# Binary layer of a vision tower: weight products on four 64x64 tiles, 512-wide sign sums, gated signs tripled through DRAM

## The reference, cut

```python
xh = layernorm(h)                                     # 64 channels a token
gate = sigmoid(xh @ proj_w.T + proj_b) > 0.5          # 8 gates a token
w = einsum("be,eio->bio", gate, weight)               # per token a 64 x 64 matrix
y = einsum("bi,bio->bo", sign(xh), sign(w)) * scale
h = h + y
```

## Time and profile before

| | |
|---|---|
| time, 3 runs | 1758.92 us median (1758.51 to 1761.61) |
| span of the profiled execution | 1762.0 us |
| PE, PEld busy | 1600.4, 1209.6 us |
| DVE, ACT, POOL busy | 1205.6, 974.5, 540.3 us |
| mean granted TensorE clock | 0.973 |
| largest line on the chain that ended last | L887, 11% |

### The profile page before, as it was taken

How to read it: one execution, slowest core, us unless ns; L and a number is a source line. 1 busy time by engine, 2 the same in 40 slices (tenths; PEclk the granted TensorE clock), 3 DMA queues, 4 the chain that set the end, 5 groups by cost and what they waited for, 6 DMA issues and landing times.

```text
span 1762.0 us, 87962 instructions
## 1 busy us (share of the span) xinstructions
PE 1600.4 (91%) x32618; PEld 1209.6 (69%) x32618; DVE 1205.6 (68%) x3509; ACT 974.5 (55%) x1893; POOL 540.3 (31%) x699
## 2 busy tenths in 40 slices
PE   6989898779999999999986899999999999999996
PEld 4666666567777777777775666766676666766663
DVE  3878787645565566655554677877778777877762
ACT  2333333234444444444432278888888878888776
POOL 2311111145555555555542212222222212222210
PEclk9999999869999999999998699999999999999999
DMA  5010101034444344443342133333333333333332
GB/s 160 26 30 24 30 24 35 2 102 107 113 114 109 105 111 115 112 115 109 106 117 56 31 81 84 85 85 86 84 83 82 89 83 83 83 85 87 84 77 61
DMA packets 134691, 143.29 MB, mean 81 GB/s; under 512 B 42498, under 2 KB 90114, under 8 KB 134370
## 3 DMA queue, kind: packets, MB, share of 16 engines
q1 hardware_dynamic: 126306, 116.16, 25.3%
q10 hardware_dynamic: 8320, 26.22, 5.2%
HBM read 66.51 MB, written 16.99 MB: 47 GB/s over the span
## 4 chain that ended last, share of the span: by engine, by line
PE 64%; issue 11%; POOL 6%; DVE 5%; SPq 4%; ACT 4%; DMA 4%; POOLq 1%; ACTq 0%; DVEq 0%
PE ps_D L887 11%; PE ps_D L798 4%; PE ps_D L675 3%; PE ps_AV L904 3%; SPq L462 3%; PE ps_J L837 3%; POOL key_patch L561 3%; DMA q_st<-q_d 3%; PE ps_J L995 2%; PE ps_J L963 2%; POOL key_patch L560 2%; DVE tile_a L1285 2%; PE ps_J L945 2%; PE ps_OT L751 2%; PE ps_OT L641 2%
## 5 line engine op out<-in xcount | busy, mean ns | idle before, releaser
L1175 ACT ACTIVATE prob<-ps_D 128x1024 bf16<-128x1024 f32 x448 | 459.5, 1029 | 123.8 <-PE ps_D L887 122.2
L1145 ACT ACTIVATE prob<-ps_D 100x512 f32<-100x512 f32 x256 | 139.0, 595 | 223.2 <-PE ps_D L798 223.2
L1349 DVE TENSOR_REDUCE m_sb<-ps_D 128x4 f32<-128x400 f32 x256 | 135.3, 570 | 126.4 <-PE ps_D L775 126.4
L798 PE MATMUL ps_D<-tile_a,key_patch 64*100 64x128 f32 x2048 | 174.2, 288 | 0.3 <-issue 0.3
L887 PE MATMUL ps_D<-tile_b,w_parts 128*128 128x256 bf16 x1024 | 151.5, 273 | 13.0 <-ACT prob L1175 3.4
L887 PE MATMUL ps_D<-tile_a,w_parts 128*128 128x256 bf16 x1024 | 152.0, 274 | 11.6 <-DVE xg L1471 2.8
L552 POOL TENSOR_TENSOR tile_a<-q_st,q_mask 128x1024 f32<-128x1024 f32 x64 | 123.5, 1930 | 61.8 <-DMA q_st<-q_d 59.5
L798 PEld LDWEIGHTS ps_D<-tile_a,key_patch 64*100 64x100 f32 x2048 | 135.7, 166 | 0.5 <-issue 0.5
L794 PE MATMUL ps_D<-mT,key_rows 64*100 64x128 bf16 x1024 | 120.9, 227 | 7.9 <-issue 7.4
L527 POOL TENSOR_TENSOR rstd_bin<-veps_bin,minus_half 128x2 f32<-128x2 f32 x64 | 44.2, 691 | 267.2 <-DVE veps_bin L1236 267.2
L887 PEld LDWEIGHTS ps_D<-tile_b,w_parts 128*128 128x128 bf16 x1024 | 92.6, 102 | 45.3 <-issue 34.3
(11 more groups left out here) (176 smaller groups left out, 3963.4 us busy)
## 6 DMA issues: line engine op xcount, KB each, us to landing
tile_a<-xg SPq DMA_DIRECT2D x384, 64.0 KB, 2.0
tile_b<-xg SPq DMA_DIRECT2D x384, 64.0 KB, 2.0
key_st<-k_d SPq DMA_DIRECT2D x128, 162.0 KB, 3.0
tile_b<-v_d ACTq DMA_DIRECT2D x128, 120.0 KB
tile_b<-v_d ACTq DMA_DIRECT2D x64, 160.0 KB
w_exp<-experts SPq DMA_DIRECT2D x64, 129.0 KB, 2.3
xT<-in_x SPq DMA_DIRECT2D x32, 256.0 KB, 2.6
k_d<-kpad SPq DMA_DIRECT2D x64, 64.0 KB, 3.0
```

The costliest lines, as they stand in the source:

```text
L798: mm = pe.matmul(s_loc[x][0:NKL, u * P:(u + 1) * P], key_patch[rows_of(x), par, at * NKL:(at + 1) * NKL], q_block[rows_of(x), par, at * P: ...
L1145: act.activation(prob1[0:NKL, 2 * g + x, :], s_loc[x][0:NKL, :], ACT.Exp).then_inc(T2["exp_done"], 1)
L1175: act.activation(sgn[:, k % 4, :], unit(k, par)[:, :], ACT.Sign).then_inc(BN["sign"], 1)
L1349: dve.tensor_reduce(m_sb[:, C * x + HOT[x] + 4 * g:C * x + HOT[x] + 4 * g + 4], m_loc[x][:, 0:4 * NKL].rearrange("p (u n) -> p u n", u=4), ...
```

## The change

- The weight products use four tiles of 64 x 64. Of 64 rows, 48 hold 3 parts of 2 channel lanes x 8 gates; the two row halves hold different channels. A unit is 8 products of 256 columns (2 output halves x 2 lane pairs x 2 row halves) instead of 4. The row half selects the PSUM bank, the lane pair the column half.
- The sign sums take 512 columns: 4 products for two units instead of 8. ysum is 512 wide, its two halves are added by L985's product, now 4 in place of 2.
- xg goes to a DRAM tensor x_d by 2 transfers of 128 KB, and after a wait for both comes back three times by 2 transfers of 384 KB with a repeating source (48 rows of 8 KB each). xg of the next strip waits for the first two only, unit 0 for a semaphore of its own for each buffer.
- The rows to be cleared are now 32 to 63 and 96 to 127 of both tiles: 4 memsets. SP waits for them before its first strip.
- DVE places the weights by 2 multiplies and 4 multiply-adds over 128 rows, with a mask for part and lane.

The diff without the changed declarations of names:

```diff
@@ -108,11 +108,11 @@
     t["keep"] = np.repeat(np.stack([keep, keep * np.float32(ALPHA ** P)])[None], P, 0)
-    group, lane, gate = np.arange(P) // 32, np.arange(P) % 32 // NG, np.arange(P) % NG
-    t["lane_mask"] = (lane[:, None] == np.arange(4)[None, :]).astype(np.float32)
+    half, part, lane = np.arange(P) // 64, np.arange(P) % 64 // 16, np.arange(P) % 16 // NG
+    t["part_mask"] = ((part[:, None, None] == np.arange(3)[None, :, None]) & (lane[:, None, None] == np.arange(2)[None, None, :])).astype(np.float32).reshape(P, 6)
     spread = np.zeros((P, 4, P), np.float32)
     for n in range(4):
-        spread[C + 16 * n + 4 * group + lane, n, np.arange(P)] = 1
+        spread[C + 32 * half + 2 * (4 * part + n) + lane, n, np.arange(P)] = 1
     t["spread"] = spread.reshape(P, 4 * P)
@@ -192,14 +192,14 @@
         x_parts = [tile_a[:, :, :].rearrange("p a n -> p (a n)").bitcast(BF16), tile_b[:, :, :].rearrange("p a n -> p (a n)").bitcast(BF16)]
-        PARTS = 96
-        w_bin, w_rest = key_patch[0:PARTS, :, :].rearrange("p a n -> p (a n)")[:, 0:1024], key_rows[0:PARTS, :, :].rearrange("p a n -> p (a n)")[:, 0:1024]
-        w_high, w_mid, w_sel = rot[0:PARTS, 0, :].bitcast(BF16), rot[0:PARTS, 1, :].bitcast(BF16), q_sb[0:PARTS, :, :].rearrange("p a n -> p (a n)").bitcast(BF16)
-        ysum, ys, yo = sb("ysum", [P, 256], BF16), sb("ys", [P, 2, C]), sb("yo", [P, 2, C])
+        w_bin, w_rest = key_patch[:, :, :].rearrange("p a n -> p (a n)")[:, 0:1024], key_rows[:, :, :].rearrange("p a n -> p (a n)")[:, 0:1024]
+        w_high, w_mid, w_low = rot[:, 0, :].bitcast(BF16), rot[:, 1, :].bitcast(BF16), q_sb[:, :, :].rearrange("p a n -> p (a n)").bitcast(BF16)
+        ysum, ys, yo = sb("ysum", [P, 512], BF16), sb("ys", [P, 2, C]), sb("yo", [P, 2, C])
 
         q_d = nc.dram_tensor("q_d", (NSTRIP, P, P), F32, kind="Internal").ap()
+        x_d = nc.dram_tensor("x_d", (NSTRIP, 2, 16, 4, 1024), BF16, kind="Internal").ap()
         o_v = out.rearrange("b (t p) c -> p (b t) c", p=P)
@@ -456,10 +456,15 @@
                 sp.wait_ge(BN["xg"], times(g + 1))
+                for half in range(2):
+                    sp.dma_start(x_d[bass.ds(g, 1), half, :, :, :].rearrange("a l g n -> g (a l) n"), xg[rows_of(half), :]).then_inc(BN["x_out"], 16)
                 sp.wait_ge(BN["w_ps"], times((g - 1) * 8))
-                for part in range(3):
-                    for n in range(4):
-                        sp.dma_start(x_parts[par][32 * part:32 * (part + 1), 1024 * n:1024 * (n + 1)], xg[32 * n:32 * (n + 1), :]).then_inc(BN["x_in"], 16)
+                sp.wait_ge(BN["x_out"], times((g + 1) * 32))
+                settle(sp)
+                for half in range(2):
+                    src = x_d[bass.ds(g, 1), half, :, :, :].rearrange("a l g n -> (a l) (g n)")
+                    src = bass.AP(src.tensor, src.offset, [[0, 3], [4096, 16], [1, 4096]])
+                    sp.dma_start(x_parts[par][C * half:C * half + 48, :], src).then_inc(BN["x_in%d" % par], 16)
 
@@ -472,6 +477,7 @@
             sp.dma_start(w_bin, a["w_bin"]).then_inc(s_gate_w, 16)
+            sp.wait_ge(s_clear, 4)
             staggered(sp, strips)
@@ -581,10 +587,11 @@
             gp.wait_ge(T2["h_done"], times(NS))
-            gp.memset(tile_a[PARTS:P, :, :], 0.0).then_inc(s_clear, 1)
-            gp.wait_ge(s_clear, 1)
-            gp.memset(tile_b[PARTS:P, :, :], 0.0).then_inc(s_clear, 1)
-            gp.wait_ge(s_clear, 2)
+            for n, (tile, at) in enumerate(((tile_a, 32), (tile_a, 96), (tile_b, 32), (tile_b, 96))):
+                if n:
+                    gp.wait_ge(s_clear, n)
+                gp.memset(tile[at:at + 32, :, :], 0.0).then_inc(s_clear, 1)
+            gp.wait_ge(s_clear, 4)
 
@@ -882,10 +889,12 @@
                     for oh in range(2):
-                        for a in range(2):
-                            at = (2 * (k % 2) + a) * 4 + k // 2
-                            mm = pe.matmul(d[:, a * 512 + oh * 256:a * 512 + (oh + 1) * 256], w_parts[:, at, oh, :, :].rearrange("r i o -> r (i o)"),
-                                           x_parts[half][:, at * 256:(at + 1) * 256], start=True, stop=True)
+                        for lanes in range(2):
+                            for x in range(2):
+                                at = 2 * k + lanes
+                                mm = pe.matmul(d[rows_of(lanes), x * 512 + oh * 256:x * 512 + (oh + 1) * 256],
+                                               w_parts[rows_of(x), at, oh, :, :].rearrange("r i o -> r (i o)"),
+                                               x_parts[half][rows_of(x), at * 256:(at + 1) * 256], start=True, stop=True)
                     mm.then_inc(BN["w_ps"], 1)
@@ -900,9 +909,10 @@
                     for k in (2 * pair, 2 * pair + 1):
-                        for cg in range(4):
-                            mm = pe.matmul(bank["AV"][32 * cg:32 * (cg + 1), 0:256], lane_sum[:, int(k == 1), :], sgn[:, k % 4, cg * 256:(cg + 1) * 256],
-                                           start=k == 0, stop=k == 7)
+                        for oh in range(2):
+                            cg = 2 * (k % 2) + oh
+                            mm = pe.matmul(bank["AV"][32 * cg:32 * (cg + 1), :].rearrange("o (x t) -> o x t", x=2), lane_sum[:, int(k == 1), :],
+                                           sgn[:, k % 4, :].rearrange("r (x h t) -> r h x t", x=2, h=2)[:, oh, :, :], start=k < 2, stop=k >= 6)
                     mm.then_inc(BN["y_part"], 1)
@@ -982,7 +992,9 @@
                     for t in range(2):
-                        mm = pe.matmul(bank["T"][:, 256 + t * C:256 + (t + 1) * C], ysum[:, t * P:(t + 1) * P], half_sum[:, :], start=True, stop=True)
+                        for x in range(2):
+                            mm = pe.matmul(bank["T"][:, 256 + t * C:256 + (t + 1) * C], ysum[:, 256 * x + t * P:256 * x + (t + 1) * P], half_sum[:, :],
+                                           start=x == 0, stop=x == 1)
                     mm.then_inc(BN["y_ps"], 1)
@@ -1040,8 +1052,8 @@
                         pe.wait_ge(s_placed, 13)
-                        pe.wait_ge(s_clear, 2)
-                    pe.wait_ge(BN["x_in"], times((n + 1) * 192))
+                        pe.wait_ge(s_clear, 4)
+                    pe.wait_ge(BN["x_in%d" % (1 - par)], times((n + 1 + par) * 16))
                 if q is not None:
@@ -1179,7 +1191,7 @@
                     act.wait_ge(BN["y_ps"], times(p))
-                    act.activation(ysum[:, :], bank["AV"][:, 0:256], ACT.Copy).then_inc(BN["ysum"], 1)
+                    act.activation(ysum[:, :], bank["AV"][:, :], ACT.Copy).then_inc(BN["ysum"], 1)
                 if f is not None or g is not None:
@@ -1413,17 +1425,18 @@
                     dve.tensor_copy(w_mid, w_rest).then_inc(s_placed, 1)
-                    dve.tensor_copy(w_sel[0:32, :], w_high[0:32, :]).then_inc(s_placed, 1)
-                if j == 2:
-                    dve.wait_ge(s_placed, 7)
-                    dve.tensor_tensor(w_sel[64:96, :], w_rest[64:96, :], w_mid[64:96, :], ALU.subtract).then_inc(s_placed, 1)
-                    dve.tensor_copy(w_sel[32:64, :], w_mid[32:64, :]).then_inc(s_placed, 1)
-                if j == 3:
-                    dve.wait_ge(s_placed, 9)
-                if j in (3, 4):
-                    for lane in (2 * j - 6, 2 * j - 5):
-                        dve.tensor_scalar(w_parts[0:PARTS, :, :, lane, :], w_sel.rearrange("p (n h o) -> p n h o", n=16, h=2),
-                                          lane_mask[0:PARTS, lane:lane + 1], None, ALU.mult).then_inc(s_placed, 1)
+                    dve.wait_ge(s_placed, 6)
+                    dve.tensor_tensor(w_low, w_rest, w_mid, ALU.subtract).then_inc(s_placed, 1)
+                if j in (2, 3, 4):
+                    for lane in range(2):
+                        dve.wait_ge(s_placed, 7 + 2 * (j - 2) + lane)
+                        dst = w_parts[:, :, :, lane, :]
+                        src = (w_high, w_mid, w_low)[j - 2].rearrange("p (n h o) -> p n h o", n=16, h=2)
+                        own = part_mask[:, 2 * (j - 2) + lane:2 * (j - 2) + lane + 1]
+                        if j == 2:
+                            dve.tensor_scalar(dst, src, own, None, ALU.mult).then_inc(s_placed, 1)
+                        else:
+                            dve.scalar_tensor_tensor(out=dst, in0=src, scalar=own, in1=dst, op0=ALU.mult, op1=ALU.add).then_inc(s_placed, 1)
 
@@ -1467,7 +1480,7 @@
                     dve.wait_ge(BN["gates"], times(g + 1))
-                    dve.wait_ge(BN["x_in"], times(g * 192))
+                    dve.wait_ge(BN["x_out"], times(g * 32))
                     dve.tensor_tensor(xg[:, :].rearrange("r (n t) -> r n t", n=4), ring(5, par)[:, :].rearrange("r (n t) -> r n t", n=4),
@@ -1547,7 +1560,7 @@
     arr["b_gate"] = np.tile(n(L1_ffn_proj_b), P // NG).reshape(P, 1)
```

(8 more changed lines are left out.)

## The result

Against 1760.06 us before (4 runs) the changed kernel takes 2405.62 us (median of 4 runs, 2404.75 to 2415.37): a ratio of 1.369, with a 95% interval of 1.366 to 1.372. Forecast was 1746, with a range of 1714 to 1777. The sign was wrong, and the size by a factor that no term of the sum comes near.

The account below looks back on a forecast made before the run. PE, busy 91% of the span, and its in-order queue were taken as the bound. 1762.0 - 15 - 4 + 6.5 = 1749.5 us for the profiled execution, whose span is 3.1 above the median, so about 1746; range 1714 to 1777.

Parts of the forecast that it names:

- Part 3: Tripling xg through DRAM: the trip takes 9.7 us, needed after 13, so hidden; -4 us in all.
- The -4 for both ends: Layer stage's first and last strips: removing the Sync loop saves 2.4 us plus the last unit 0's 1.41 us wait.
- The Sync loop of 11.3 to 12.2: Kernel before: xg, its 12 transfers and their landing take this many us a strip, hidden behind PE except in the last strips.
- Part 1: Weight products as 64x64 tiles: w4 and w7 lose 0.09 us each, w5 and w6 gain 0.11 each, w0, w1, w3 gain.
- Rival 2: Weight products on PE: entering 64x64 tiles costs 0.1 us more in five places, total 1777 us; chance 0.22.
- rival 4: Weight products on PE: only two quadrants run together, 1.2 us more a strip, 1823 us; chance 0.04.
- Part 2: Sign sums 512 wide: sums within 0.02 us of zero, y products +0.06 on PE, ysum +0.21 on ACT.
- The walk: One strip followed step by step: L945 waits for ACT's xs and leads only 0.3 to 0.35 us; period falls 0.24.
- The state step: DVE's step L1487 after xg: L1037 waits for it, leads only 0.2 to 0.3 us and starts 0.11 slower.
- Part 4: Way into the layer stage: two more memsets +3.7 us, DVE's weight placing +2.8, together +6.5.
- -15: Middle of the layer stage: 64 strips, each 0.24 us shorter, save 15 us.
- rival 5: DRAM trip: it takes over 13 us and unit 0 waits in each strip; chance 0.02.

Follow-up runs that it names:

- e5: Changed kernel with the three copies as inner dimension of the return transfers and xg sent out in one 128-row transfer: 1747.47 us, ratio 0.9954.
- e3: Kernel before, 128x128 weight products kept, with xg sent to DRAM in one transfer and back in three, 32 rows outermost: 1745.6 us, ratio 0.9917.
- e7: e6 with the sign sums as before the change, 8 products of 256 columns and ysum 256 wide: 1729.69 us, ratio 0.9854.
- e6: e5 with each tile cleared by one memset over all 128 rows, two instead of four: 1745.8 us.
- e1: Changed kernel with xg sent out in one 128-row transfer and back in six, 16 rows outermost: 1750.01 us, ratio 0.9939.
- e8: e6 with ScalarE's order xfgT, xs, ysum instead of ysum, xfgT, xs: 1741.29 us, ratio 0.9921.
- e10: e7 with ScalarE's order xfgT, xs, ysum, as in e8: 1723.0 us, ratio 0.9819.
- e2: Changed kernel with rows outermost on the way back from DRAM only, the way out left as in the change: 1840.58 us (one run).
- e9: Changed kernel with only the way out to DRAM altered, to one transfer of 128 rows: 2289.0 us, ratio 1.3037.

## Why the prediction was wrong, point by point

**Part 3, the step that failed.** "From the end of xg: 1.4 + 1.1 + 3 + 1.1 + 3.1 = 9.7 us, and w0 needs it 13 us after", hidden "with about 3 us of cover". The 2.7 (3 in the sum) and 3.1 were landings of other transfers, v_d<-v_sb and the load of w_bin, taken over by their bytes alone. The 384 KB of w_bin have 96 rows outermost, those of x_in three copies. In the change the two trips take 11.9 and 17.9 us. The dimension order was in the diff. Two errors lie in that step:
- the landing of x_in: 17.9 for 3.1. Even well shaped it is 5.7 (e5), with 768 KB a strip under way and not the 384 of that row;
- transfers were priced as if each had the engines to itself. x_out, w_exp and the store stand behind x_in in the engines that it fills. "Behind the waiting Sync stand w_exp and the store of y, both due a strip later: hidden" looked at Sync's issue order only, not at what is under way.

With good shapes the step holds: in e5 the trip fits and nobody waits for it. The -4 for both ends was too small. e3, which changes only this, has the same 11.64 us in its middle, but from its first to its last clip (1015.5 to 1739.1) 723.6 us for 732.8. 8.0 of these 9.2 lie in the last seven strips, 71.7 us for 79.7. Whole layer stages, from the first memset on, are 793.2 and 803.0 us: the ends are worth 9.8. The Sync loop of 11.3 to 12.2 held more of the last strips than the xg steps showed.

**Part 1, the units.** Right within 0.02. From start to start, w4: L973 to the unit 0.60 (L963 before: 0.51), the unit 0.34 (0.44), L983 0.54 (0.43), 1.48 for 1.38: it loses 0.10, and 0.09 was forecast. w7 loses 0.10. w5 and w6 gain 0.10 each, for 0.11. From the product ahead of w0 to the sums behind w1 the way is 0.92 for 1.28, a gain of 0.36, for 0.34. A unit is 8 products in 0.34 us, the price of the L904 block (0.33). Rival 2, dearer entries, and rival 4, two quadrants at a time, fall. e7 against e3 is this part alone in the middle of the stage, where neither waits for a transfer: 11.64 to 11.24, 0.40 us a strip.

**Part 2, the sums.** L985 (L996 now) +0.06 as forecast: 0.21 to the next start, 0.15 with two products. ysum 0.59, as taken from L1145. The walk's "new wait, for ACT" is there, 0.35 at L955. Together they take back 0.22 of the 0.40 (e7 to e6). The forecast had 0.24 left, the measurement 0.18.

**The state step** was to gate L1037. It doesn't: in e1 the unit ahead of it (w7) takes 0.34 like the others, and L1049 (L1037 before) starts behind it without a wait for DVE.

**Part 4, the way in.** From the first memset to the first clip pass 58.2 us before, 57.9 in e3, 62.4 in e5 and 63.8 in e1: 4 to 6 us more, for 6.5 forecast. The memsets are 2.6 of it (e6), for 3.7. The rest is taken for DVE's placing, which no run shows apart: e6, with two memsets as in e3, needs 59.9, 1.9 more than e3, for 2.8 forecast; e7, e8 and e10, which place alike, are 0.3 to 2.2 above e3. The first xg was to come 6 us later; from the first memset it is 3.4 later in e5 and 4.8 in e1.

**The sum.** -15, -4 and +6.5 were forecast, -12.5 together; the repaired change measures 7 to 10 less than before (e5, e1). That is close, but by terms that don't agree: e3 alone, the transfers without the tiles, already has 14.8 less (1745.6 against 1760.41), and the tiles with their wide sums add nothing to it. From layer stage to layer stage, e1 against e3: the first 56 periods give 9.7, the way in takes 5.9 more (63.8 for 57.9), the last seven strips 3.2 more (74.9 for 71.7) and what follows the last clip 1.3 more: together 0.6 more by the unrounded times, 793.8 for 793.2 us. The spans, 1749.5 and 1750.7, have it the other way, since the layer stage began 1.9 earlier in e1; neither edit touches what lies before it. So the 10 us that the middle gives are spent at the two ends. The last one has a term that the forecast lacks. The last stretches of e3, and under them of e1 (columns as above):

```profile
1700.00:1715.00 15.00, 14.56 (x139) 9.59 (x141) 9.10 (x29) 12.14 (x19) 1.38 (x2) 1.00 0.48 124
1715.00:1730.00 15.00, 12.18 (x125) 6.37 (x126) 6.83 (x16) 12.60 (x16) 0.69 (x1) 1.00 0.47 111
```

```profile
1700.00:1715.00 15.00, 11.86 (x158) 6.64 (x161) 7.98 (x22) 11.25 (x15) 1.31 (x2) 1.00 0.61 114
1715.00:1730.00 15.00, 12.33 (x141) 4.80 (x139) 4.65 (x6) 12.03 (x15) 0.00 (x0) 0.65 0.49 93
```

With faster units PE has less to do while the pipeline runs empty, 11.86 of 15 us for 14.56, and then its granted clock falls, 0.65 for 1.00. In e5 and e6 it falls earlier: it is 0.84 and 0.75 from 1685 to 1700 us, and two strips there take 13.8 and 13.9 us in e5, 13.3 and 14.0 in e6, for 11.5. That the lighter load is the cause is argued from these rows; no run held the clock.

**Chances.** 0.02 for rival 5 rested on a cover of 3 us that was computed from landings of other shapes. A cost that no row shows had been given a single value, and no upper bound.

## What to carry to other kernels

Price a transfer by its access pattern, not by its bytes: write down the outermost size of source and destination, and look for a row with the same. A broadcast dimension belongs inside, behind a dimension of 16 rows as in e5. And a long transfer on few engines delays each later transfer of the queue, small ones too; a landing time that grew for a transfer nobody touched is the sign of it.

## What the runs showed of the hardware

- 768 KB in 96 packets of 8 KB take 17.9 us on three engines and 5.7 on sixteen (the 384 KB rows of e5). The gain is 3.1-fold, less than the 16/3 of the engines, and a packet itself is slower with sixteen at work: by the packet records from 1100 to 1700 us it takes 0.45 us on average in the changed kernel and 0.70 in e5, where sixteen at a share of 0.89 give 180 GB/s.
- 256 KB out to DRAM in 128 packets of 2 KB: 2.0 us with 128 rows outermost (325 GB/s at a share of 0.84), 4.0 with four outermost (e2, where the DMA share is 0.25 from 1497 to 1500 us, four engines of 16).
- The granted clock falls to the lower level, 1.2 GHz, when PE waits: in e9 it is 1.00 up to 1512, though PE has stopped soon after 1510, and 0.54 over the next 6 us, in which PE does nothing. There it costs nothing: the next x_out is issued at 1530.47, some 8 us before the x_in that it stands behind is in. At the end of a repaired kernel it may (e1 against e3).
- Clearing 2048 f32 a row takes POOL 1.80 us over 32 rows (e3) and 1.80 over 128 (e6).
- 64x64 tiles in four quadrants run together: 8 products of 256 columns in 0.34 us, with 0.09 more on the block ahead and 0.10 on an f32 block behind (e1).
